# Attention and mixture of experts on one core: slot rows turned by VectorE, an expert's weights asked for in halves

## The reference, cut to what matters

```python
x = L0_attn_x                                   # (4, 512, 512) f32
x = layernorm(x + attention(x, Wq, Wk, Wv, Wproj, ...))      # 16 heads of 128, ALiBi, RMS-normed q, k, y
# the mixture of experts, on x_flat (2048, 512):
router_logits = x_flat @ w_router               # (2048, 8)
top_vals, top_idx = jax.lax.top_k(router_logits, 2)
probs = jax.nn.softmax(top_vals, axis=-1)
w_tok = zeros((N, E)).at[rows, top_idx].add(probs)
h = jnp.einsum('nc,ecd->ned', x_flat, w_fc)     # w_fc (8, 512, 512)
h = jnp.square(jax.nn.relu(h))
y = jnp.einsum('ned,edc->nec', h, w_proj)       # w_proj (8, 512, 512)
out = jnp.einsum('nec,ne->nc', y, w_tok)
x = layernorm(x + out)
```

## Time and profile before

| | us |
|---|---|
| median of 3 runs | 1440.74 (1440.17 to 1444.86) |
| the profiled execution, its own time | 1442.51 |
| its span on the core | 1440.7 |
| TensorE busy in the span | 1400.9 (97%) |
| VectorE / ScalarE / GpSimd busy | 813.3 / 730.3 / 424.2 |
| mean busy share of the DMA engines, 1190 to 1350 us | 0.65 |

### The profile page before, as it was taken

The page is one execution under the profiler, slowest core; times in us unless marked ns, Lnnn a source line. Parts: engine busy times, 40 slices in busy tenths (PEclk is TensorE's granted clock), DMA queues, the critical chain, the costliest instruction groups (busy, mean ns, idle before and its releaser), DMA issues. The chain is left out here.

```text
span 1440.7 us, 26432 instructions
## 1 busy us (share of the span) xinstructions
PE 1400.9 (97%) x7744; PEld 1184.6 (82%) x7745; DVE 813.3 (56%) x1877; ACT 730.3 (51%) x1633; POOL 424.2 (29%) x410
## 2 busy tenths in 40 slices
PE   8999999999999999999999999999999989999994
PEld 6888888888888888888888888878887868888783
DVE  6555655656556555555565555567777763333334
ACT  5565656656556566566565565543333223333334
POOL 1212221212112122222121212103445553353565
PEclk9999999999999999999999999999999999999997
DMA  5243333232433333333334245557659546756699
GB/s 185 75 130 95 109 95 115 88 113 91 131 95 109 95 96 108 96 107 109 117 89 115 76 128 157 143 136 171 148 137 233 176 139 247 265 201 230 187 192 237
DMA packets 136851, 200.45 MB, mean 139 GB/s; under 512 B 16624, under 2 KB 83312, under 8 KB 133488
## 3 DMA queue, kind: packets, MB, share of 16 engines
q1 hardware_dynamic: 126032, 149.67, 36.0%
q0 software_dynamic: 10784, 50.36, 11.9%
HBM read 160.05 MB, written 92.62 MB: 175 GB/s over the span
## 5 line engine op out<-in xcount | busy, mean ns | idle before, releaser
L413 POOL TENSOR_TENSOR small<-small,half 128x4 f32<-128x4 f32 x193 | 195.0, 1010 | 764.2 <-DVE small L443 764.2
L557 DVE CUSTOM_DVE_ANT_0 logit<-score_ps,bias 128x128 f32<-128x128 f32 (+3 forms) x256 | 124.8, 487 | 157.1 <-PE score_ps L699 117.6
L347 ACT ACTIVATE prob<-logit,small 128x128 f32<-128x128 f32 (+3 forms) x256 | 144.2, 563 | 120.1 <-DVE small L557 116.5
L712 PEld LDWEIGHTS y_ps<-vs,prob_t 128*128 128x128 f32 x1280 | 175.1, 191 | 21.5 <-ACT prob_t L354 4.5
L712 PE MATMUL y_ps<-vs,prob_t 128*128 (+1 forms) x1280 | 185.6, 276 | 0.7 <-ACT prob_t L354 0.7
L354 ACT ACTIVATE prob_t<-prob_ps 128x128 f32<-128x128 f32 (+3 forms) x256 | 111.5, 436 | 54.9 <-PE prob_ps L705 53.9
L705 PE MATMUL prob_ps<-ident,prob 128*128 128x128 f32 x640 | 112.8, 274 | 3.2 <-ACT prob L347 2.8
L443 DVE TENSOR_REDUCE small<-squares 128x4 f32<-128x516 f32 x128 | 88.4, 691 | 45.7 <-ACT squares L269 43.8
L631 PE MATMUL v_ps<-w_hi,x_hi 128*128 (+1 forms) x256 | 106.7, 417 | 1.4 <-DVE w_lo L488 1.4
L929 ACT ACTIVATE yt_hi<-x_raw,subln 128x512 fp32r<-128x512 f32 x60 | 43.2, 723 | 126.2 <-DVE x_raw L1025 51.2
L631 PE MATMUL v_ps<-w_hi,x_lo 128*128 (+1 forms) x256 | 106.6, 416 | 0.0
(11 more groups left out here) (233 smaller groups left out, 3370.0 us busy)
## 6 DMA issues: line engine op xcount, KB each, us to landing
slots_x<-in_zeros SPq DMA_DIRECT2D x64, 512.0 KB, 4.4
y_scratch<-x_now SPq DMA_DIRECT2D x65, 256.0 KB, 2.8
x_raw<-in_x_t SPq DMA_DIRECT2D x64, 256.0 KB, 2.6
slots_y<-in_zeros SPq DMA_DIRECT2D x64, 256.0 KB, 4.4
y_raw<-y_scratch SPq DMA_DIRECT2D x56, 256.0 KB
w_raw<-in_w_experts POOLq DMA_DIRECT2D x7, 2048.0 KB
w_hi<-in_w_experts POOLq DMA_DIRECT2D x7, 2048.0 KB
w_raw<-in_w_all SPq DMA_DIRECT2D x16, 768.0 KB, 6.1
```

The source lines that it names most:

```text
L347: nc.scalar.activation(prob[:, 0:width], logit[:, 0:width], ACT.Exp, scale=-1.0, bias=least[:, h:h + 1], accum_out=row_sum[:, (i % 2) * HG ...
L413: nc.gpsimd.tensor_tensor(r, ms, half[:, :], ALU.pow).then_inc(ready, 1)
L557: nc.vector.tensor_tensor_reduce(out=logit[:, 0:width], in0=score_ps[:, 0:width], in1=bias[:, h, T - width:T], scale=1.0, scalar=3e38, op0 ...
L712: mm = nc.tensor.matmul(y_ps[:, :].rearrange("p (b h i) -> p h b i", b=QB, h=HG)[:, h, :, :], prob_t[:, j * P:(j + 1) * P], one(vs[:, bass ...
```

## The change: what it does

1. Slot rows are turned by VectorE. `turn_x` moves from `slots_tensor` to `slots_vector`: one `nc.vector.transpose` of 128x512, which transposes each 32x32 block. So that this gives channel-major rows, a load now brings four pieces, one for each group of 32 partitions, in runs of 128 channels (512 bytes): `load_row_blocks` issues four transfers of 64 KB in place of one of 256 KB. The rows of `w_fc` are permuted on the host accordingly. The result (`xt`) lies in SBUF instead of PSUM.
2. Four row buffers (`YB`) instead of two; two of them are `res` and `x1_t`. SP asks for the rows of tile k+6 in step k. Of tile 2, the first whose place the tables tell, ScalarE asks for half of the pieces.
3. The order on ScalarE and VectorE within a step: `round_x` stands before `rectify`, `split_x` before `square`, and `turn_x(k+3)` at the end of VectorE's step. On VectorE `row_places` stands before the turning of tile 2.
4. GpSimd asks for raw weights in halves. In the middle of the eight subtractions of turn e it asks for the first raw half of turn e+1, waits until turn e-2 is done, and asks for the rounded weights of turn e+1; behind the eighth it asks for the second raw half.
5. The filling transposes before up(2), `keep_busy`, are 46 instead of 10.

```diff
-        xs, hid, yo = y_raw[:, 0, 0:2, :], y_raw[:, 0, 2:4, :], y_raw[:, 1, :, :]
+        xs = (y_raw[:, 0, 0, :], y_raw[:, 0, 1, :], res[:, :], x1_t[:, :])
+        hid, yo = y_raw[:, 0, 2:4, :], y_raw[:, 1, :, :]
...
+        def load_row_blocks(engine, at, y, blocks):
+            for u in blocks:
+                engine.dma_start(xs[y][u * QP:(u + 1) * QP, :].rearrange("p (a c) -> p a c", a=QB),
+                                 x_slots[bass.ds(at, 1), u, :, :, :].rearrange("o j a c -> (o j) a c"))\
+                    .then_inc(xs_loaded[y], 16)
...
             def slot_step(k, b, h, y, q):            # SP
+                if more(k, 6):
+                    ahead_at = tile_at(k + 6)
+                    sp.wait_ge(xs_turned, k + 3)
+                    sp.nop(nofuse=True)
+                    load_rows(ahead_at, (y + 2) % YB)
                 if more(k, 4):
                     at = tile_at(k + 4)
-                if more(k, 4):
-                    sp.wait_ge(xs_turned, k + 3)
-                    sp.nop(nofuse=True)
-                    load_rows(at, b)
...
+                    if s == WT // 2 - 1 and ahead is not None:      # GpSimd, split_turn
+                        nxt = expert_of(ahead)
+                        pool.wait_ge(we_split, WT * e + WT // 2)
+                        pool.nop(nofuse=True)
+                        load_raw_half(nxt, 0)
+                        if end is not None:
+                            pool.wait_ge(down_done, end)
+                            pool.nop(nofuse=True)
+                        load_rounded(ahead, nxt)
                 pool.wait_ge(we_split, WT * e + WT)
+                pool.nop(nofuse=True)
+                if ahead is not None:
+                    load_raw_half(nxt, 1)
...
             def slot_step(k, b, h, y, q):            # ScalarE
                 round_hid(b, k)
+                if more(k, 2):
+                    act.wait_ge(up_done, k + 1)
+                    round_x(b, k + 3)
                 if more(k, 1):
                     rectify(1 - b, k + 1)
-                if more(k, 2):
-                    round_x(b, k + 3)
                 scale_out(k, b, y, q)
...
+            def turn_x(b, y, loaded, split=None):    # VectorE
+                dve.wait_ge(xs_loaded[y], loaded)
+                if split is not None:
+                    dve.wait_ge(xt_ready, split)
+                nc.vector.transpose(turned_columns(xt[b]), xs[y]).then_inc(xs_turned, 1)
...
             def slot_step(k, b, h, y, q):            # VectorE
                 split_hid(b, k)
+                if more(k, 2):
+                    split_x(b, k + 3)
                 if more(k, 1):
                     square(1 - b, k + 2)
-                if more(k, 2):
-                    split_x(b, k + 3)
+                if more(k, 3):
+                    turn_x(1 - b, (y + 3) % YB, (q + 1 + (y + 3) // YB) * (16 * QB), k + 2)
...
-            keep_busy(h_ps[1], 10)                   # TensorE
+            keep_busy(h_ps[1], 46)
             up(0, second, 3)
-            turn_x(1, 32)

             def slot_step(k, b, h, y, q):
                 turn_hid(b, k)
                 if more(k, 1):
                     up(1 - b, load_owner(k + 1), k + 2)
-                if more(k, 2):
-                    turn_x(b, h * 16 + 32)
                 down(b, load_owner(k), k)
```

More of the change, by code:

```diff
@@ L864, in ps @@
             return ctx.enter_context(nc.psum_tensor(name, [P, C], F32))
-        turn_ps = [ps(f"turn_ps{g}") for g in range(NHG)]
+        h_ps = [ps("h_ps0"), ps("h_ps1")]
         out_ps = [out_first, ps("out_ps1")]
@@ L1326, in mixture_phase @@
         g_loaded = [sem(f"g_loaded{y}") for y in range(YB)]
+        last_projected = sem("last_projected")
         we_cast = sem("we_loaded")
-        xs_loaded = [sem("xs_loaded0"), sem("xs_loaded1")]
+        raw_half = [raw_loaded, sem("raw_second_half")]
+        xs_loaded = [sem(f"xs_loaded{y}") for y in range(YB)]
         xs_turned, xt_rounded, xt_ready = sem("xs_turned"), sem("xt_rounded"), sem("xt_ready")
@@ L1362, in tile_at, with load_rows @@
             def tile_at(k):
[L1363 to L1367, removed]
+                return tile_of_turn(sp, k)
+            def load_rows(at, y, blocks=range(QB)):
+                load_row_blocks(sp, at, y, blocks)
             def load_gates(at, y):
@@ L1387, in slots_sync @@
             for k in range(HEAD, YB):
-                sp.wait_ge(xs_turned, k - 1)
-                load_rows(tile_at(k), k % 2)
+                load_rows(tile_at(k), k, range(QB // 2) if k == HEAD else range(QB))
             for b in range(2):
@@ L1393, in slots_sync @@
                 load_gates(tile_at(k), k)
+            for k in range(HEAD):
+                sp.wait_ge(xs_turned, k + 1)
+                load_rows(tile_at(k + YB), k)
             def slot_step(k, b, h, y, q):
+                if more(k, 6):
[3 more added lines that the diff above has]
+                    load_rows(ahead_at, (y + 2) % YB)
                 if more(k, 4):
                     at = tile_at(k + 4)
[L1398 to L1401 removed]
                 sp.wait_ge(yo_ready, k + 1)
@@ L1416, in slots_gpsimd, with expert_of, load_rounded @@
         def slots_gpsimd(pool, token_step, inverse_std, dispatch, send_gates):
-            def load_turn(e, end, raw=True):
+            def expert_of(e):
                 at = turn_i[0:1, e:e + 1] if isinstance(e, int) else turn_i[0:1, bass.ds(e, 1)]
[L1420 to L1425, removed]
+                return rows_of(w_experts[bass.ds(pool.value_load(at, min_val=0, max_val=E - 1), 1), :, :])
+            def load_rounded(e, src):
                 blk = expert_block(e)
@@ L1428, in load_turn, with load_raw_half, split_turn @@
                 pool.dma_start(hi.rearrange("p s f -> p (s f)"), src).then_inc(we_cast, 16)
-            def split_turn(e):
+            def load_raw_half(src, half):
+                part = slice(half * (WT // 2), (half + 1) * (WT // 2))
+                pool.dma_start(w_raw[:, part, :].rearrange("p s f -> p (s f)"),
+                               src[:, part.start * F:part.stop * F]).then_inc(raw_half[half], 16)
+            def split_turn(e, ahead, end):
                 blk = expert_block(e)
-                pool.wait_ge(raw_loaded, 16 * e)
+                pool.wait_ge(raw_half[0], 16 * e)
                 pool.wait_ge(we_cast, 16 * e)
                 for s in range(WT):
+                    if s == WT // 2:
+                        if not (isinstance(e, int) and e == 1):
+                            pool.wait_ge(raw_half[1], 16 * e - 16)
                     hi, lo = (w[:, blk + s, :] if isinstance(e, int) else one(w[:, bass.ds(blk + s, 1), :])
@@ L1528, in slots_scalar @@
             scale_out(0, 0, 0, 0)
+            act.wait_ge(tables_known, 1)
+            for b in range(2):
+                act.wait_ge(dispatched[b], 32 * (NT // 2))
+            load_row_blocks(act, tile_of_turn(act, HEAD), HEAD, range(QB // 2, QB))
             round_x(0, 3)
@@ L1621, in slots_vector @@
             layernorm(NT - 2, 0, 16 * NT - 32)
+            dve.wait_ge(yt_ready, NT * NHG)
+            turn_x(0, 0, 16 * QB)
             split_x(0, 1)
+            turn_x(1, 1, 16 * QB)
             split_x(1, 2)
```

48 lines of the change are left out of this document (24 added, 24 removed).

## The result

| | before | after |
|---|---|---|
| median of runs on the same chip, us | 1441.83 (1440.17 to 1444.86) | 1453.19 (1449.21 to 1453.99) |
| the profiled execution, us | 1442.51 | 1449.21 |
| its span, us | 1440.7 | 1447.1 |

Four runs of each; the ratio after to before is 1.0071, 95% interval 1.0045 to 1.0097. The forecast was 1428.1 and faster; the kernel is slower, and the time is outside the range.

A forecast was written before the change was run, and what follows sets the result against it. TensorE, busy 97% of the span, was taken to bound the kernel. Gains of 13.6 + 1.5 + 0.5 less 3.0 gave 12.6 us, so a median of 1440.74 - 12.6 = 1428.1 us, range 1422.5 to 1436.

The forecast's parts named there:

- The step of 6.03: In the slots, one step between turn_hids on TensorE was to take 6.03 us, against 6.47 before.
- (a, b): Slots: steps 3 to 33 each lose a turn_x on TensorE, 13.6 us; and the wait for rows goes, 1.5 us.
- the turning's 0.70: Turning the rows in the slots was to give VectorE about 0.7 us more work per step.
- up(2) at 1177.3: Tile 2's up product on TensorE was to start at 1177.3, 1.1 us later than before.
- (e) Weights in halves: GpSimd's last four subtractions of each turn wait behind down of turn e-2: cost nothing, about 1 us if one tile.
- (c) The seam: From the last token tile's projections into the first slot steps: gain between +1.4 and -0.4 us, taken as 0.5.
- Rival D: VectorE's square and split_x each wait a whole GpSimd subtraction of 1.3 us: 6 us lost, 1434; chance 0.05.
- (d) Tile 5: Tile 5's rows land late beside turn 2's weights, so TensorE stands still once before down(3): 3 us lost.
- The end: Second gathers start from about 1383, one every 1.85 us; the kernel ends a fixed 45 us after tile 33 is stored.
- C: Late stores make GpSimd's first gathers end late, second gathers start right behind them: 6 us lost, 1434; chance 0.07.
- E: Every burst of weights holds the rows back and VectorE holds TensorE: 27 us slower, 1468; chance 0.07.

The follow-up runs named there:

- one stop: The changed kernel with one GpSimd stop: sixth subtraction waits for the fifth (0.9967, 1436.25 us), or a stop between the requests and the run (0.9964, 1437.27 us).
- three stops: The changed kernel, but each of the last three subtractions of a turn waits on the semaphore of the one before: 0.9946, 1433.17 us.

## Why the prediction was wrong, point by point

- *The step of 6.03* (a, b): right. So were the turning's 0.70, the row wait that goes, and up(2) at 1177.3 (it was 1177.08).
- *The step that failed* is "(e) Weights in halves ... Cost nothing". I moved a request into the subtractions and looked at its transfers, not at what the run behind it does to VectorE. The 15.0 us of the five turns are its price, besides a part of the 4.8 in the seam, and they go with one stop: the time is then 0.3 to 0.5% under the kernel before.
- *(c) The seam* was mis-sized: 4.8 us later than forecast. The square caught for 5.78 is part of it, and up(2) to down(2) takes 14.3 us; but with three stops it still takes 12.9, where the forecast had 9.3. The sum let square go on "as before" and left out that the split_x of tile 3 behind it can now wait for subtractions as well. With three stops both waited, and up(3) took 5.1 us at the lower clock, more than the dearer of the two values (4.6) that the prediction had weighed.
- *Rival D* had the right pair of engines and the wrong duration. It allowed each wait "a whole subtraction of 1.3", from square's 1.18. "Up to 1.18" holds only for those rows: the same trace has a square of 1.76 at 1323.17, which still fits a wait for one subtraction. Every run of before began behind a wait, so none could show the other case. By four subtractions, 5.03, it would have been slower. The Trainium skill (SBUF — State Buffer, "Who interferes with whom") says that the engine which comes second is blocked for the whole instruction of the other. The traces agree for runs that begin behind a wait (at most 1.84); behind a request the block lasted up to four instructions.
- *(d) Tile 5*: right as a mechanism, wrong as one number. I took 3 us; it cost TensorE nothing in the changed kernel and 4.2 in another run, and was not there in the trace of the kernel that asks for the weights later.
- *The end*: the second gathers were taken at 1.85 each, as nothing of before departed from it. They took 1.98. This is C's place, and its sign (second gathers right behind the first), with another cause: the locks that made the first gathers late, and two-operand work of VectorE that slowed them, not late stores. With the lock gone (three stops) the second gathers started at 1383.71 against 1382.7 forecast, and their fifteen beats took 2 us more than forecast.
- *E*, the only slower rival, blamed rows behind every burst of weights. VectorE waited for rows 1.5 us in all, so that the kernel came out slower was E's forecast, but not for E's cause.
- What remains open: why a request has this effect on the run behind it (the runs show that it does and what ends it); whether it has to be a request, since no run here began without a stop behind anything else; and whether a request by another engine would have it too. Neither was tried.

## What to carry to other kernels

Where two engines can shut each other out, a mean and a maximum read from one pattern of issue do not bound another: ask what stands directly ahead of the run, and whether it stops there. A change that releases two engines by the same event fixes their phase, so a collision comes back in every round. And when the bounding engine is made faster, work out the next one's whole chain, with its durations beside the new neighbours.

## What the runs showed of the hardware

- A run of GpSimd subtractions directly behind a DMA request of its own keeps a VectorE operation with two SBUF inputs out until the run ends: four subtractions cost 4.8 to 5.8 us when it comes at their start, and 2.8 to 3.2 when it comes in their middle. With a stop of 0.1 to 0.3 us on a semaphore behind the request, or behind the first subtraction, it gets in after about one (1.0 to 2.15). A request with no run behind it holds up nothing (0.69).
- Operations that read PSUM (0.69) are not held up in either case. The block transpose took 0.70 beside runs with a stop or behind a wait; none fell into a run that locked.
- The reverse holds for GpSimd's indirect gathers, which take 1.54 alone: one that starts 0.05 us into such an operation takes 2.07, at 0.26 it is 1.83, at 0.36 1.75, and from 0.6 on 1.54 again. Three that started 0.00 to 0.03 into one took 1.54 as well.
